# The last block's probabilities in a buffer and on two queues of their own, and another order behind the last loop

## The reference

```python
for layer in range(6):
    q, k, v = split(x @ Wqkv)                      # 16 heads of 64
    q, k = rotate(l2norm(q) * qs), rotate(l2norm(k) * ks)
    sim = einsum(q, k of own and previous window) * 8      # windows of 32 tokens
    x = x + (softmax(masked sim) @ v) @ Wo
    xn = layernorm(x) * g + b
    a, gate = split(xn @ W1 + b1)                  # 341 columns each
    x = x + (a * gelu(gate)) @ W2 + b2
```

## Time and profile before

| | |
|---|---|
| median of 3 runs | 1872.35 us (1867.59 to 1873.53) |
| the profiled execution | 1872.07 us |
| its span, first to last instruction | 1870.3 us |
| mean granted TensorE clock | 0.969 of full |
| busy in the span: PE, DVE, ACT, POOL | 94%, 82%, 62%, 66% |
| share of PE in the chain that ended last | 75% |

### The profile page before, as it was taken

One profiled execution on the slowest core, in us unless ns is written; L12 is line 12 of the kernel. 1 busy time (PEld: TensorE's weight loads), 2 busy tenths in 40 slices (PEclk: granted clock), 3 DMA queues, 4 the chain that ended last, 5 costly groups with the idle time before them and its releaser, 6 DMA issues.

```text
span 1870.3 us, 72882 instructions
## 1 busy us (share of the span) xinstructions
PE 1749.8 (94%) x31224; PEld 1184.1 (63%) x31224; DVE 1536.5 (82%) x2117; ACT 1151.5 (62%) x2221; POOL 1236.1 (66%) x789
## 2 busy tenths in 40 slices
PE   7699987899999999999999999999999999999975
PEld 2255553566667666666667676666767666666653
DVE  6599847888888888888888888889888988898853
ACT  5633214576676767676767676667666767676742
POOL 2477733877676767676767676767676767676730
PEclk9799967999999999999999999999999999999996
DMA  4535000233322233322333223332223322222220
GB/s 98 135 54 69 12 3 23 59 85 89 91 75 70 70 98 90 82 70 70 87 90 93 70 70 82 93 91 74 70 70 98 90 80 72 65 74 66 72 63 23
DMA packets 73442, 137.29 MB, mean 73 GB/s; under 512 B 18528, under 2 KB 24096, under 8 KB 72864
## 3 DMA queue, kind: packets, MB, share of 16 engines
q1 hardware_dynamic: 73120, 132.63, 27.7%
HBM read 29.79 MB, written 2.10 MB: 17 GB/s over the span
## 4 chain that ended last, share of the span: by engine, by line
PE 75%; issue 3%; DVE 3%; SPq 1%; DMA 0%; ACT 0%; POOL 0%; DVEq 0%; ACTq 0%; POOLq 0%
PE bank L1380 16%; PE bank L1453 10%; PE bank L1393 9%; PE bank L1470 9%; PE bank L1385 8%; PE bank L1428 8%; PE bank L1487 7%; PE bank L1511 3%; PE bank L1415 2%; PE bank L1477 2%; DVE ff_T L1832 1%; PE bank L1481 1%; SPq L1258 1%; DMA p_T<-p_blocks 0%; DVE rot L1780 0%
## 5 line engine op out<-in xcount | busy, mean ns | idle before, releaser
L1780 DVE TENSOR_TENSOR rot<-bank,gains 128x1024 f32<-128x1024 f32 x384 | 466.6, 1216 | 121.6 <-ACT squares L1613 115.0
L1324 POOL TENSOR_TENSOR rot<-rot,rnorm 128x1024 f32<-128x1024 f32 x192 | 361.3, 1903 | 288.2 <-ACT rnorm L1623 275.1
L1318 POOL TENSOR_TENSOR rot<-rot 128x1024 f32<-128x1024 f32 x192 | 455.9, 2374 | 75.0 <-DVE rot L1780 74.8
L1380 PE MATMUL bank<-wqkv,x 128*128 128x512 f32 x768 | 396.0, 609 | 8.3 <-DVE rot L1780 4.6
L1613 ACT ACTIVATE squares<-bank 128x512 f32<-128x512 f32 x384 | 230.2, 600 | 254.9 <-PE bank L1380 248.0
L1654 ACT ACTIVATE o_T<-bank 128x512 f32<-128x512 f32 x192 | 104.2, 598 | 210.9 <-PE bank L1453 210.8
L1342 POOL TENSOR_TENSOR probs<-probs,total 128x1024 f32<-128x1024 f32 x96 | 182.8, 1905 | 71.7 <-DVE total L1808 71.7
L1786 DVE TENSOR_REDUCE rnorm<-squares 128x16 f32<-128x1024 f32 x192 | 227.6, 1186 | 0.2 <-issue 0.2
L1453 PEld LDWEIGHTS bank<-p_T,v_shift 64*64 64x64 f32 x6144 | 165.5, 135 | 64.8 <-issue 58.1
L1393 PE MATMUL bank<-st_ident,rot 128*128 128x128 f32 x1536 | 203.1, 275 | 2.0 <-issue 1.2
L1393 PEld LDWEIGHTS bank<-st_ident,rot 128*128 128x128 f32 x1536 | 176.7, 142 | 43.6 <-issue 28.3
(11 more groups left out here) (198 smaller groups left out, 2861.0 us busy)
## 6 DMA issues: line engine op xcount, KB each, us to landing
p_T<-p_blocks SPq DMA_DIRECT2D x768, 64.0 KB
v_shift<-v_tok SPq DMA_DIRECT2D x96, 384.0 KB, 3.5
v_shift<-v_tok SPq DMA_DIRECT2D x96, 128.0 KB, 3.6
wqkv<-in_wqkv SPq DMA_DIRECT2D x36, 256.0 KB
v_rep_sb<-v_by_step SPq DMA_DIRECT2D x32, 128.0 KB
v_rep<-v_by_step SPq DMA_DIRECT2D x32, 128.0 KB
wo<-in_wo SPq DMA_DIRECT2D x12, 256.0 KB
w<-in_w SPq DMA_DIRECT2D x6, 341.0 KB
```

Source lines behind the costliest of these rows:

```text
L1318: nc.gpsimd.tensor_tensor(out=out, in0=out, in1=halves_of, op=ALU.add).then_inc(rot_added.sem, 1)
L1324: nc.gpsimd.tensor_tensor(out=by_head(qk[u][:, half]), in0=by_head(qk[u][:, half]), in1=rnorm[u][:, AH * i:AH * (i + 1)].unsqueeze(2).to_b ...
L1380: nc.tensor.matmul(QK_BANKS[i][:, :], shifted_tokens(x, n, P), layer_cols(wqkv, n, 3 * INNER, 512 * i, 512), start=True, stop=True).then_i ...
L1780: nc.vector.tensor_tensor(both, src.unsqueeze(1).to_broadcast([P, 2, 8, DH]), pair_of_gains.unsqueeze(2).to_broadcast([P, 2, 8, DH]), ALU. ...
```

## The change

The change has three parts.

1. **The last block's probabilities.** `turn_p(LAST)` writes to `last_blocks`, which is the first half of `squares`, so it waits for the last reader of `squares` and not for the landing of `p_blocks`. A new semaphore `last_placed` counts the eight DMAs. SyncE issues the four of windows 0 and 1, ScalarE those of windows 2 and 3 (`place_last`). `outputs(LAST)` waits for the new semaphore.
2. **Free banks for the last two pairs.** `gate_place` and `a_place` say where each part of gate and a goes. For pair m-1 the gate's tail goes to bank 6 and a's parts 0 and 1 to bank 7. For pair m they go to bank 0 and bank 1. These parts need no read of the gate first. Only a's tail waits for the first gelu pair.
3. **Another order behind the loop**, on TensorE, ScalarE and VectorE.

```diff
--- before.py
+++ after.py
@@ -1129,6 +1129,7 @@
     v_shift = two("v_shift", (P, INNER))
     probs, p_T = two("probs", (P, PAIRS, 2, DH)), two("p_T", (P, 2, AH, WINDOW))
     p_blocks = sb("p_blocks", (P, 2, AH, WINDOW))
+    last_blocks = squares[:, 0:INNER].rearrange("p (g h k) -> p g h k", g=2, k=WINDOW)
     o_T = sb("o_T", (P, PAIRS, PT))
     peak, total = two("peak", (P, 2, PAIRS)), two("total", (P, AH))
 
@@ -1150,6 +1151,7 @@
     rotated, rot_added, ss_made, above_floor = sig("rotated", per=4), sig("rot_added", per=2), sig("ss_made", per=2), sig("above_floor")
     rnorm_log, rnorm_made, qk_made, v_read = sig("rnorm_log"), sig("rnorm_made"), sig("qk_made", per=2), sig("v_read", per=2)
     v_placed, p_placed = sig("v_placed", per=2 * 16), sig("p_placed", per=2 * WINDOWS * 16)
+    last_placed = sig("last_placed", per=2 * WINDOWS * 16, credit=0)
     q_turned, qT_made, k_turned, kT_made, halo_made = sig("q_turned", per=2), sig("qT_made", per=2), sig("k_turned", per=2), sig("kT_made", per=2), sig("halo_made")
     s_product, peak_made, shifted, exp_made = sig("s_product"), sig("peak_made", per=2), sig("shifted", per=2), sig("exp_made")
     total_made, p_normed, p_turned = sig("total_made", per=2), sig("p_normed"), sig("p_turned")
@@ -1184,6 +1186,20 @@
 
         return BESIDE_FF_BANK if m == LAST_PAIR - 1 else FF_BANK
 
+    TAIL_BANKS = {LAST_PAIR - 1: (T_BANKS[1], T_BANKS[0]), LAST_PAIR: (LAST_S_BANKS[1], LAST_S_BANKS[0])}
+
+    def gate_place(m, i):
+
+        if m in TAIL_BANKS and i == 2:
+            return TAIL_BANKS[m][1][:, 0:PT]
+        return ff_bank(m)[:, PT * (i % 2):PT * (i % 2 + 1)]
+
+    def a_place(m, i):
+
+        if m not in TAIL_BANKS:
+            return ff_bank(m)[:, PT * (i % 2):PT * (i % 2 + 1)]
+        return ff_bank(m)[:, 0:PT] if i == 2 else TAIL_BANKS[m][0][:, PT * i:PT * (i + 1)]
+
     def layer_cols(tile, n, width, at=0, size=None):
 
         return tile[(n // BLOCKS) % 2][:, at:at + (width if size is None else size)]
@@ -1226,6 +1242,16 @@
             sp.dma_start(tile[:, :], a[name][ds(layer, 1), :].to_broadcast([P, c1])).then_inc(w_loaded.sem, 16)
         else:
             sp.dma_start(tile[:, c0:c1], a[name][ds(layer, 1), :, c0:c1].rearrange("l p n -> p (l n)")).then_inc(w_loaded.sem, 16)
+
+    def place_last(queue, first, end):
+
+        queue.wait_ge(p_turned.sem, p_turned.after(LAST))
+        queue.wait_ge(o_product.sem, o_product.after(LAST - 2))
+        for w in range(first, end):
+            for half in range(2):
+                row = DH * (w // 2) + WINDOW * half
+                queue.dma_start(p_T[LAST % 2][row:row + WINDOW, w % 2, :, :],
+                                last_blocks[WINDOW * w:WINDOW * (w + 1), half, :, :]).then_inc(last_placed.sem, 16)
 
     def load_early(sp):
 
@@ -1282,7 +1308,7 @@
         place_p(LAST - 2)
         place_p(LAST - 1)
         place_v(LAST)
-        place_p(LAST)
+        place_last(sp, 0, WINDOWS // 2)
 
         def store(n0, n1):
             sp.wait_ge(f_normed.sem, n1)
@@ -1442,7 +1468,10 @@
                     pe.wait_ge(shifted.sem, shifted.after(n))
                 pe.wait_ge(v_read.sem, v_read.after(n))
                 pe.wait_ge(v_placed.sem, v_placed.after(n))
-                pe.wait_ge(p_placed.sem, p_placed.after(n))
+                if n == LAST:
+                    pe.wait_ge(last_placed.sem, last_placed.after(0))
+                else:
+                    pe.wait_ge(p_placed.sem, p_placed.after(n))
             for a_ in (2 * q, 2 * q + 1):
                 for turn_ in range(2):
                     v = v_tok[n % V_SLOTS] if turn_ else v_shift[n % 2]
@@ -1480,29 +1509,36 @@
             pe.wait_ge(cent_squared.sem, cent_squared.after(m))
             nc.tensor.matmul(ff_bank(m)[:, PT:2 * PT], mean_ones[:, :], cent_sq[:, :], start=True, stop=True).then_inc(var_product.sem, 1)
 
-        def up(m, parts, at, made):
-
-            for j, i in enumerate(parts):
+        def up(m, parts, at, made, place):
+
+            for i in parts:
                 f0, size = FF_PARTS[i]
-                mm = nc.tensor.matmul(ff_bank(m)[0:size, PT * j:PT * (j + 1)], layer_cols(w1, PAIR * m, 2 * FF, at + f0, size), xn_T[:, :],
+                mm = nc.tensor.matmul(place(m, i)[0:size, :], layer_cols(w1, PAIR * m, 2 * FF, at + f0, size), xn_T[:, :],
                                       start=True, stop=True)
             mm.then_inc(made.sem, 1)
 
         def up_gate_full(m):
             pe.wait_ge(xnT_made.sem, xnT_made.after(m))
-            up(m, (0, 1), FF, gate_product)
+            up(m, (0, 1), FF, gate_product, gate_place)
 
         def up_gate_tail(m):
-            pe.wait_ge(gate_made.sem, gate_made.after(m, 2))
-            up(m, (2,), FF, gate_product)
+            if m in TAIL_BANKS:
+                pe.wait_ge(oT_made.sem, oT_made.after(LAST - 1 if m < LAST_PAIR else LAST))
+            else:
+                pe.wait_ge(gate_made.sem, gate_made.after(m, 2))
+            up(m, (2,), FF, gate_product, gate_place)
 
         def up_a_full(m):
-            pe.wait_ge(gate_made.sem, gate_made.after(m))
-            up(m, (0, 1), 0, a_product)
+            if m not in TAIL_BANKS:
+                pe.wait_ge(gate_made.sem, gate_made.after(m))
+            up(m, (0, 1), 0, a_product, a_place)
 
         def up_a_tail(m):
-            pe.wait_ge(ff_made.sem, ff_made.after(m, 2))
-            up(m, (2,), 0, a_product)
+            if m in TAIL_BANKS:
+                pe.wait_ge(gate_made.sem, gate_made.after(m, 2))
+            else:
+                pe.wait_ge(ff_made.sem, ff_made.after(m, 2))
+            up(m, (2,), 0, a_product, a_place)
 
         def down(m):
             pe.wait_ge(ff_made.sem, ff_made.after(m))
@@ -1543,7 +1579,7 @@
 
         def final_turn(part):
             n0, n1 = FINAL_PARTS[part]
-            pe.wait_ge(oT_made.sem, oT_made.after(LAST - 1))
+            pe.wait_ge(oT_made.sem, oT_made.after(LAST - 2))
             if part >= 2:
                 pe.wait_ge(f_added.sem, part - 1)
             pe.wait_ge(x_ready.sem, x_ready.after((DEPTH - 1) * BLOCK_PAIRS + n1 // PAIR - 1))
@@ -1575,21 +1611,21 @@
+        final_turn(0)
+        variances(m - 1)
         attend(outputs, LAST - 1)
-        variances(m - 1)
+        final_turn(1)
         attend(outputs, LAST)
         up_gate_full(m - 1)
-        final_turn(0)
-        final_turn(1)
+        up_gate_tail(m - 1)
+        up_a_full(m - 1)
...
@@ -1677,7 +1713,7 @@
             size, col = FF_PARTS[i][1], (m // BLOCK_PAIRS) * 2 * len(FF_PARTS) + len(FF_PARTS) + i
             act.wait_ge(gate_product.sem, gate_product.after(m, 1 + i // 2))
             act.wait_ge(ff_made.sem, ff_made.after(m - 1))
-            nc.scalar.activation(gate_T[0:size, i, :], ff_bank(m)[0:size, PT * (i % 2):PT * (i % 2 + 1)], ACT.Gelu,
+            nc.scalar.activation(gate_T[0:size, i, :], gate_place(m, i)[0:size, :], ACT.Gelu,
                                  bias=b1[0:size, col:col + 1]).then_inc(gate_made.sem, 1)
 
         def gelu_full(m):
@@ -1731,8 +1767,9 @@
         gelu_full(m - 2)
         gelu_tail(m - 2)
         logs_and_exps(m - 2)
+        exponent(LAST)
         read_o(LAST - 2)
-        exponent(LAST)
+        place_last(act, WINDOWS // 2, WINDOWS)
         square_cent(m - 1)
         inverse_sigma(m - 1)
         affine(m - 1)
@@ -1810,8 +1847,11 @@
         def turn_p(n):
 
             dve.wait_ge(p_normed.sem, p_normed.after(n))
-            dve.wait_ge(p_placed.sem, p_placed.after(n - 1))
-            nc.vector.transpose(p_blocks[:, :, :, :], probs[n % 2][:, :, :, :].rearrange("t a p (g k) -> t g (a p) k", k=WINDOW)).then_inc(p_turned.sem, 1)
+            if n == LAST:
+                dve.wait_ge(ss_made.sem, ss_made.after(n))
+            else:
+                dve.wait_ge(p_placed.sem, p_placed.after(n - 1))
+            nc.vector.transpose(last_blocks if n == LAST else p_blocks[:, :, :, :], probs[n % 2][:, :, :, :].rearrange("t a p (g k) -> t g (a p) k", k=WINDOW)).then_inc(p_turned.sem, 1)
 
         def add_attention(m):
             dve.wait_ge(y_product.sem, y_product.after(m))
@@ -1829,7 +1869,7 @@
             dve.wait_ge(a_product.sem, a_product.after(m, 1 + i // 2))
             dve.wait_ge(gate_made.sem, gate_made.after(m, i + 1))
             dve.wait_ge(y2_product.sem, y2_product.after(m - 1))
-            nc.vector.scalar_tensor_tensor(out=ff_T[0:size, i, :], in0=ff_bank(m)[0:size, PT * (i % 2):PT * (i % 2 + 1)],
+            nc.vector.scalar_tensor_tensor(out=ff_T[0:size, i, :], in0=a_place(m, i)[0:size, :],
                                            scalar=b1[0:size, col:col + 1], in1=gate_T[0:size, i, :],
                                            op0=ALU.add, op1=ALU.mult).then_inc(ff_made.sem, 1)
 
@@ -1898,25 +1938,25 @@
+        turn_p(LAST - 1)
+        totals(LAST)
         gated_full(m - 2)
-        turn_p(LAST - 1)
         gated_tail(m - 2)
-        totals(LAST)
+        turn_p(LAST)
...
```

(15 more changed lines are left out.)

6 lines of the change are left out of this document (2 added, 4 removed).

## The result

The changed kernel takes 1862.05 us (median of 14 runs, 1853.19 to 1866.67), beside 1870.95 us for the kernel before in the same series (14 runs, 1863.0 to 1876.06). The ratio is 0.995, with a 95% interval of 0.9935 to 0.9965, so 8.9 us faster (6.5 to 12.2). The forecast was 1856.4, with a range of 1852.5 to 1862. The direction was right. The gain was forecast at 15.7 us, which is 1.8 times the 8.9 measured, and the measured time lies at the very end of the range. The profiled execution took 1864.6, with a span of 1862.8.

What follows compares the result with a forecast made beforehand. It saw the end behind the loop bound by two successive hauls, one-bank waits and a falling clock. Gains of 8.2 (outputs(LAST)) and 8.5 (up to down(m-1)), less 1.0 (pair m), made 15.7: 1872.1 - 15.7 = 1856.4, range 1852.5 to 1862.

Steps and rivals of the forecast that it cites:

- The haul and the transposes: Behind the loop: turn_p(LAST) no longer waits for the first haul and starts at 1807.35, where it started at 1813.05.
- outputs(LAST-1) 1812.95 to 1814.95 ... outputs(LAST) to 1817.4 at full clock: TensorE's last two groups of outputs: the second ends at 1817.4 instead of 1825.6, 8.2 us earlier.
- From there to the end of the last down: Stretch from the end of outputs(LAST), 1817.4, to the end of down(m), 1839.9, with low clock in pair m.
- Gate, tail and a without a wait: TensorE in pair m-1: three banks let gate, gate's tail and a run without a wait, from 1817.4 to 1819.6.
- 1.0 given back in pair m, where VectorE's final norm now stands in the way: Last pair: VectorE's final_norm (3.16) and final_add(3) (1.15) precede gated_full(m), costing 1.0 us of the gain.
- The second queue: ScalarE issues four of the last block's eight DMAs; were that worthless, the sum would be 1.2 us smaller.
- The sum: Whole tail: down(m) ends at 1839.9 instead of 1855.6, 15.7 us less, or 18.8 if the clock holds.
- A: Rival: ScalarE's queue or the handovers are slow, taking 3 to 7 us of the gain: 1859 to 1863; chance 0.12.
- B: Rival: the clock is low from 1815 on, costing 11.5 us: 1868, no measurable change; chance 0.05.
- the clock is 0.50 before 1825: Sign named as showing the forecast wrong: the granted clock at half before 1825 us from the span's start.
- C: Rival: slower, ScalarE's four DMAs go one by one at several us each; 1879 at 6 us each; chance 0.03.
- D: Rival: the change doesn't do what it says, outputs(LAST) waits for v_shift instead; 1856 to 1858; chance 0.01.

Runs made afterwards that it cites:

- e2: The changed kernel, unedited, run again for a second profile; the changed kernel's ratio to the kernel before was 0.9957 in that timing.
- e6: Changed kernel with 4 of the 12 blocks' final normalisation moved behind add_ffn and final_add(3) behind the gated product; ratio to the kernel before 0.9923, 1853.75 us.
- e9: Changed kernel with the first 12 blocks' final work moved into VectorE's idle stretch ahead of add_attention(m); 1852.74 us, ratio to the kernel before 0.9914.
- e3: Changed kernel with all eight DMAs of the last block on SyncE; ratio to the kernel before 0.9961.

## Why the prediction was right or wrong

*The haul and the transposes*: right to 0.1 us on VectorE (5.2 for 5.3 behind S). Outputs of LAST no longer wait for p_T.

*"outputs(LAST-1) 1812.95 to 1814.95 ... outputs(LAST) to 1817.4 at full clock"*: this is the step that was furthest off. I priced each group at the 2.04 of the earlier trace rows and started the first at S + 10.9, which was right. They took 3.3 to 3.9 each, so outputs of LAST ended at S + 18.6 to 18.9 instead of 15.3: 3.3 to 3.6 us too little in the sum. A group of outputs is 256 instructions long, so every group meets the end of a line; 2.04 is what it takes where the next line is there by then, and most of the 96 groups in the trace before are like that (median 2.07). But five of them in the loop, from 357, 701, 1044, 1387 and 1735 us on, took 2.8 to 3.5 with such a stall, and the forecast had no such price. With the new order both closing groups are of that kind. In the kernel before, the second group ran at half clock in 3.64 and could not show it.

*From there to the end of the last down*: 22.5 forecast; 20.6, 23.8 and 21.8 measured. Right, in part by luck. I took the clock as low in the last pair, and it was low, high or in between by execution, and in e2 low in pair m-1 as well.

*Gate, tail and a without a wait*: right, 2.35 for 2.17, and the gain hangs on it: putting the old banks back takes all of it.

*"1.0 given back in pair m, where VectorE's final norm now stands in the way"*: right in kind, and too small. Freed, the last pair gives 3 to 4 us (e6, e9), since the last down then also runs at a higher clock.

*The second queue*: nothing instead of 1.2, since the stall ahead of the outputs of LAST hides it. The Trainium skill, in "DMA: Bandwidth & Descriptors", section Issuing engines are not separate DMA queues, says that issuing from several engines saves only the time of issuing. e3 agrees, with 0.9961 on one queue beside 0.9957 on two: here the issue time itself was off the path.

*The sum*: 15.7 forecast for the tail. Of this 3.4 went in the outputs. Another 1.0 is the profile that I summed against (53.5, where the mean of three is 52.5). With 0.4 won back behind the outputs, the tails of three profiles each give 11.7. The timed difference is 8.9, with 12.2 as its upper end. The other 2.8 are within what the interval and the spread of S leave open; no run here says where they would be.

*Rivals*: A (ScalarE's queue) did not come about; its four issues took 0.78 each. Yet the measured 1862.05 lies in the 1859 to 1863 that A gave: the time alone would have taken the stalls for a slow queue. (A was weighed with seven of eight issues at the median; the earlier trace rows and the chain behind it have six, one of 1.54 and one of 0.51. The range was said to reach to the middle of A, which is 1861, and was set at 1862.) B (low clock) came in part: in e2 for 6 us behind the outputs, not the whole stretch, and with it the sign "the clock is 0.50 before 1825". C and D did not.

## What to carry to other kernels

Before a row's duration is used at a new place, look at all the groups of its kind in the trace, and not at one: the same group of 256 short TensorE instructions took 2.0 us at most places and 2.8 to 3.9 at some, above all where it filled a line of instructions nearly alone. Between two such groups 2.2 us of long multiplications delayed the second group's end by only 0.7 to 1.0. Where several results of a pipeline's end share one PSUM bank, give them free banks first, since each reuse there is a round trip between engines with nothing to hide it. And when an end has been pulled together, look for final work that can go into the engine's remaining idle stretch; here it took 3 to 4 us out of the last pair, beside 8.9 for the whole change.
